# A decoder's second self-attention: last norm by pairs, output weights rounded earlier, and some diagonals made by VectorE

## The chip, the cores and the metric

One core of a Trainium2 chip runs the whole kernel in one launch. TensorE (PE) multiplies; VectorE (DVE), ScalarE (ACT) and GpSimd (POOL) compute elementwise; SyncE (SP) issues most of the DMAs, ACT and POOL some. Each engine runs its own instructions in order and waits on semaphores. The metric is the device time of one execution in microseconds, less is better; the time of the kernel before is the median of three runs.

## The reference

Two post-norm decoder layers on x of 8 sequences x 128 tokens x 256 features, with a context of the same shape. Each layer is self-attention, cross-attention and a feed-forward part, each followed by `x = layernorm(x + part)`. Layer 0 has its own kinds of these. The part that matters here is layer 1:

```python
def _L1_attn_ref(x, w_qkv, w_o):            # 16 heads of 128, no mask
    q, k, v = split(x @ w_qkv)
    scores = einsum('bhqd,bhkd->bhqk', q, k) / sqrt(128)
    probs = softmax(scores)
    values = einsum('bhqk,bhkd->bhkd', probs, v)   # v times the column sums of probs
    return values @ w_o
def _L1_xattn_ref(q, k, v):                 # 8 heads of 16 rows, q = x, k = v = context
    sm = softmax(einsum('bdm,bdn->bmn', qh, kh) * scale)
    return einsum('bmn,bcn->bcm', sm, vh)
def _L1_ffn_ref(x, gate_w, w13, w2):        # 64 experts, the best 8 of each token
    ...
```

In the attention `values` sums probs over the queries only, so a head gives `v` times a column sum.

## The kernel before, in words

Each engine's program is a chain of stages: layer 0, attention 1, cross 1, experts, combine. There is no scheduler: the order on each engine is the order of the code, and semaphores (`t.name(n)`: wait until n events) tie the engines together.

**Attention 1** (`pe_attention1`, `act_attention1`, `dve_attention1`, `pool_attention1`, `sp_attention1`, L758 to L966) loops over 16 heads, for all 8 sequences at once in two halves of 4. Products that need full precision are made of three fp32r products, of a rounded part `_hi` and a rest `_lo`. In a head TensorE makes the scores (L814), adds the head before to the output (`add_head`, L794), projects q and k of the next head, makes the column sums (L824), and projects v of the next head. ScalarE copies `sums`, rounds `oT` to `o_hi` (L874) and, last, `wo` to `wo_hi` (L876). VectorE multiplies `oT` and makes `o_lo` (L929). GpSimd makes `w_lo` of the next head and `wo_lo`. The output of all heads stands in the PSUM banks 0 to 3, a pair of sequences in each. After the last head VectorE adds each bank to `x_all` (L935) and takes statistics (L938); then come eight aggregates (L941), the variance of all (L943), one root on GpSimd (L966), and eight normalizations (L946), which give the events `x4`.

**Cross 1** (L1072 to L1381) goes by quarters: a sequence has four, 32 in all. The engines run over slots `s` of the same number: scores of quarter s, maxima (`topc`, L1252) of s, exponentials (`softc`, L1210) of s, the reciprocal of the row sums (`rsumc`, L1257) of s-1, a diagonal matrix of them (`diagc`, L1372, on GpSimd) of s-1, the turn of s-2 (softc times diagc, which transposes and scales), and its copies (`pTc`, L1264 and L1218). At fixed slots later come values, residual and norm, the gate's logits (L1313), the choice of experts (`choose`, L1271), the place of each token (`place`, L1284, which ends with `index_all`, L1294), and the scatters of the rows into the slots of the experts: 8 indirect DMAs a sequence, issued by GpSimd, two a slot (L1363). GpSimd's program per slot is: diagonal, root of a norm (slots 7+4b), scatters (slots 13+4b to 16+4b). TensorE's bank for `topc` is one of 0 to 3.

GpSimd's set-up of cross 1 (`pool_cross1_setup`: clears `kpair` and `vpair`, makes constants) stands behind attention 1, SP's loads of the context (8 DMAs for `kpair` and one for `ctx` a sequence) wait for it, and `pe_cross1` begins when all eight `x4` are there. The experts wait until all scatters have landed.

Of the kernel before, what the change touches and what calls it, by code (L numbers as in the profile page):

```python
# [719 lines left out]
class Attention1:  # L720
    def __init__(self, m):
# [31 lines left out]
        self.var_set, self.x4 = ev.compute("dve", "var_set", 1), ev.compute("dve", "x4", NSEQ)  # L753
        self.w_lo_set, self.wo_lo_set = ev.compute("pool", "w_lo_set", 3 * H1), ev.compute("pool", "wo_lo_set", H1)
        self.root = ev.compute("pool", "root4", 1)


def sp_attention1(m, a, t, te):  # L758
# [73 lines left out]
def act_attention1(m, t):  # L832
# [24 lines left out]
    for h in range(H1):  # L857
# [18 lines left out]
        act.copy(t.wo_hi[:, :], t.wo[:, :]).then_inc(*t.wo_hi_set.one)  # L876
# [4 lines left out]
def dve_attention1(m, t):  # L881
# [17 lines left out]
    for h in range(H1):  # L899
# [30 lines left out]
        if h < H1 - 1:  # L930
            half0(h + 1, 2, t.vT)
    for k in range(4):
        x = m.x_all[:, 2 * k:2 * k + 2, :].rearrange("p b d -> p (b d)")
# [8 lines left out]
    dve.wait_ge(*c)  # L942
    dve.tensor_scalar(t.var[:, :], t.mv[:, :, 1], EPS, None, ALU.add).then_inc(*t.var_set.one)  # L943
    dve.wait_ge(*t.root(1))
    for b in range(NSEQ):
        dve.tensor_scalar(m.x_all[:, b, :], m.x_all[:, b, :], t.mv[:, b, 0:1], t.rstd[:, b:b + 1],  # L946
                          ALU.subtract, ALU.mult).then_inc(*t.x4.one)


def pool_attention1(m, t):  # L950
# [13 lines left out]
def pool_attention1_root(m, t):  # L964
    m.pool.wait_ge(*t.var_set(1))
    m.pool.tensor_tensor(t.rstd[:, :], t.var[:, :], m.power[:, 0:NSEQ], ALU.pow).then_inc(*t.root.one)  # L966
# [40 lines left out]
class Cross1:  # L1007
# [18 lines left out]
    def signals(self, m):  # L1026
        ev = m.ev
        self.gate_in = ev.dma("gate_in", 1)
# [13 lines left out]
        self.setup, self.diag_set, self.root5 = ev.compute("pool", "setup", 1), pool("cdiag", 4), pool("root5", 1)  # L1042
# [28 lines left out]

def sp_cross1(m, a, t, r, te, t1):  # L1072
    sp = m.sp
    sp.wait_ge(*t.setup(1))
    for b in range(NSEQ):
        n, L = b % LANES, t.lanes[b % LANES]
        if b >= LANES:
            sp.wait_ge(*t.cs_ps(8 * (b - 1)))
        for h in range(HX):
            rows = slice(h * HDX, (h + 1) * HDX)  # L1080
            sp.dma_start(L.kpair[rows, h % 2, :], a["ctx_in"][b, rows, :]).then_inc(*t.kpair_in[n].one)
        if b >= LANES:
            sp.wait_ge(*t.ctxT_ps(b - 1))
        sp.dma_start(L.ctx[:, :], a["ctx_in"][b, :, :]).then_inc(*t.ctx_in[n].one)
        if b == 0:
            sp.dma_start(r.gate[:, :, :], a["gatew"]).then_inc(*t.gate_in.one)
        if b == 1:
            after_attention1(sp, t1)
        if b >= 1:
            sp_kept_weights(m, a, te, b)  # L1090


def pe_cross1(m, t, r, t1):
    pe, mm, tr = m.pe, m.mm, m.tr
    pe.wait_ge(*t.setup(1))
    pe.wait_ge(*t1.x4(NSEQ))

    def scores(s):
        b, mo, g0 = quarter(s)
        L = t.lanes[b % LANES]  # L1100
        pe.wait_ge(*t.xq(b + 1))
# [141 lines left out]
def dve_cross1(m, t, r):  # L1243
# [111 lines left out]
def pool_cross1(m, t, r, t0):  # L1355
# [10 lines left out]
    for s in range(CROSS_SLOTS + 3):  # L1366
        if 0 <= s - 1 < QUARTERS:
            q = s - 1
            pool.wait_ge(*t.inv(q + 1))
            if q >= 2:  # L1370
                pool.wait_ge(*t.cT_ps(2 * (q - 2) + 2))
            pool.tensor_tensor(t.diag[q % 2][:, :, :], spread(m.ident[:, :], 4, 1), spread(t.rsum[q % 3][:, :], P, 2),  # L1372
                               ALU.mult).then_inc(*t.diag_set.one)
# [476 lines left out]
class Stages:  # L1850


    def __init__(self, m, ctx):
# [14 lines left out]
        self.tc.signals(m)  # L1868
# [63 lines left out]
```

## Time and profile before

| | us |
|---|---|
| median of 3 runs | 1078.04 |
| lowest, highest | 1076.23, 1080.29 |
| the profiled execution | 1069.34 |
| its span, first to last instruction | 1067.8 |
| TensorE busy | 842.4 (79%) |
| VectorE busy | 618.8 (58%) |
| GpSimd busy | 354.0 (33%) |
| ScalarE busy | 344.5 (32%) |
| attention 1, by the timeline | about 344 to 602 |
| cross 1, to the landing of its last scatter | about 602 to 773 |
| experts and combine | about 773 to 1068 |

A stage's share of the engines says little by itself: the engines take turns, and what counts is which wait ends last at each place. Times in the rows are microseconds from the start of the span.

### The profile page before, as it was taken

How to read it: one execution, taken by the hardware profiler on the slowest of the kernel's cores; microseconds unless marked ns; L12 is line 12 of the kernel's file. 1: busy time of each engine (PE TensorE's matmuls, PEld its weight loads, DVE VectorE, ACT ScalarE, POOL GpSimd, SP SyncE). 2: the span in 40 equal slices, each digit the busy share in tenths (PEclk: the TensorE clock that was granted, in tenths of full speed). 3: DMA queues.
4: the chain of work that ended last, by engine and by line, in shares of the span. 5: the costliest groups of instructions: out<-in, count | busy, mean ns of one | idle time of the engine just before them, and what ended most of it. 6: DMA issues, size and time to landing. Idle time of an engine off the chain costs nothing.

```text
span 1067.8 us, 16943 instructions
## 1 busy us (share of the span) xinstructions
PE 842.4 (79%) x5555; PEld 689.6 (65%) x5555; DVE 618.8 (58%) x1857; ACT 344.5 (32%) x946; POOL 354.0 (33%) x396
## 2 busy tenths in 40 slices
PE   5377888879786999999998599896099988899700
PEld 2256766557455888888887376664088877788600
DVE  4184564673853566666667567785155555544477
ACT  0032222232222343444434266663033333333200
POOL 1121312312211211222111325776645555555501
PEclk9998998998988999999999699998589999999955
DMA  9900000000000112221110233461248788854254
GB/s 238 334 11 10 1 11 11 1 20 1 1 1 34 58 43 69 70 70 52 53 41 11 67 110 100 149 236 69 109 116 281 241 260 247 285 145 135 83 209 143
DMA packets 62533, 110.12 MB, mean 103 GB/s; under 512 B 11227, under 2 KB 41417, under 8 KB 61040
## 3 DMA queue, kind: packets, MB, share of 16 engines
q1 hardware_dynamic: 32064, 64.22, 19.1%
q10 hardware_dynamic: 21216, 27.48, 8.6%
q0 software_dynamic: 9168, 17.35, 4.4%
q8 instruction: 45, 0.74, 0.3%
q14 instruction: 40, 0.33, 0.1%
HBM read 94.50 MB, written 35.52 MB: 122 GB/s over the span
## 4 chain that ended last, share of the span: by engine, by line
PE 60%; issue 13%; DVE 11%; POOL 6%; ACT 3%; DMA 2%; ACTq 1%; SPq 1%; another core or an unknown queue 1%; DVEq 0%; POOLq 0%
PE ps L152 57%; PE ps L155 4%; DVE acco L1778 3%; POOL kheads L677 2%; POOL x_slots L1363 2%; ACTq L447 1%; DVE soft L551 1%; DMA bdn_sb<-in_bdn 1%; DVE top L549 1%; SPq L286 1%; POOL mv L169 1%; DVE topc L1252 0%; DMA rowso<-y_slots 0%; POOL mvo L169 0%
## 5 line engine op out<-in xcount | busy, mean ns | idle before, releaser
L1723 POOL DMA_INDIRECT y_slots<-o_e,index_e x127 | 124.4, 979 | 116.6 <-DVE o_e L1712 80.2
L152 PE MATMUL ps<-xT_e,w_slot 128*128 128x128 f32 x760 | 101.7, 277 | 3.6 <-ACT xT_e L1662 2.1
L1704 DVE TENSOR_TENSOR h_e<-ps,gate_e 128x128 f32<-128x128 f32 x127 | 37.0, 291 | 108.2 <-ACT gate_e L1668 66.7
L152 PEld LDWEIGHTS ps<-xT_e,w_slot 128*128 128x128 f32 x760 | 92.4, 192 | 5.7 <-ACT xT_e L1662 3.2
L152 PEld LDWEIGHTS ps<-diagc,softc 128*128 128x128 f32 x512 | 62.2, 199 | 33.0 <-POOL diagc L1372 25.0
L152 PE MATMUL ps<-diagc,softc 128*128 128x128 f32 x512 | 68.2, 289 | 8.7 <-DVE pTc L1264 4.9
L1662 ACT COPY xT_e<-ps 128x256 f32<-128x256 f32 x127 | 47.2, 372 | 82.1 <-PE ps L155 63.1
L959 POOL TENSOR_TENSOR wo_lo<-wo,wo_hi 128x256 fp32r<-128x256 f32 x15 | 14.0, 932 | 176.0 <-ACT wo_hi L876 176.0
L1210 ACT ACTIVATE softc<-ps,topc 128x256 f32<-128x256 f32 x128 | 59.0, 476 | 40.4 <-DVE topc L1252 36.6
L152 PE MATMUL ps<-w_slot,h_e 128*128 128x256 f32 x190 | 59.5, 395 | 14.4 <-DVE h_e L1704 8.6
L1363 POOL DMA_INDIRECT x_slots<-rows_all,index_all x64 | 63.8, 997 | 18.0 <-issue 15.9
L155 PE MATMUL ps<-ident,rows_e 128*128 128x128 f32 x254 | 49.5, 277 | 21.9 <-DMA rows_e<-x_slots 21.9
L677 POOL TENSOR_TENSOR kheads<-k,headmask 128x1024 f32<-128x1024 f32 x16 | 38.1, 2404 | 86.3 <-ACT k L457 86.3
L1668 ACT ACTIVATE gate_e<-ps 128x128 f32<-128x128 f32 x127 | 35.5, 279 | 96.0 <-PE ps L152 88.7
L152 PE MATMUL ps<-x_hi,w_hi 128*128 128x512 f32 x192 | 61.8, 404 | 5.2 <-POOL w_lo L955 5.2
L169 POOL TENSOR_TENSOR mv<-mv,power 128x1 f32<-128x1 f32 x24 | 13.2, 548 | 157.6 <-DVE mv L165 157.6
L152 PE MATMUL ps<-x_lo,w_hi 128*128 128x512 f32 x192 | 59.8, 393 | 0.0
L152 PE MATMUL ps<-x_hi,w_lo 128*128 128x512 f32 x192 | 59.7, 392 | 0.0
L155 PEld LDWEIGHTS ps<-ident,rows_e 128*128 128x128 f32 x254 | 35.8, 143 | 34.4 <-DMA rows_e<-x_slots 22.1
L1712 DVE COPY o_e<-ps 128x256 f32<-128x256 f32 x127 | 52.9, 417 | 3.4 <-issue 1.5
L1252 DVE TENSOR_REDUCE topc<-ps 128x2 f32<-128x512 f32 x64 | 41.0, 684 | 17.9 <-PE ps L152 17.7
L1372 POOL TENSOR_TENSOR diagc<-ident,rsumc 128x512 f32<-128x512 f32 x32 | 33.3, 1041 | 45.2 <-DVE rsumc L1257 44.2
(263 smaller groups left out, 2015.1 us busy)
## 6 DMA issues: line engine op xcount, KB each, us to landing
w_slot<-in_we SPq DMA_DIRECT2D x71, 384.0 KB
rows_e<-x_slots SPq DMA_DIRECT2D x69, 136.0 KB
w_slot<-in_we ACTq DMA_DIRECT2D x24, 384.0 KB
x_slots<-blank ACTq DMA_DIRECT2D x4, 2176.0 KB, 15.8
rowso<-y_slots SPq DMA_DIRECT2D x8, 1024.0 KB, 5.0
rows_e<-x_slots ACTq DMA_DIRECT2D x58, 136.0 KB
w_kept<-in_we SPq DMA_DIRECT2D x20, 384.0 KB
wh<-in_wqkv SPq DMA_DIRECT2D x16, 384.0 KB, 3.4
```

The costliest lines, as they stand in the source:

```text
L152: return self.pe.matmul(out, lhsT, rhs, start=start, stop=stop, skip_group_check=shared)
L155: return self.pe.transpose(out, in_, self.ident[:, :])
L677: pool.tensor_tensor(L.kheads[:, mo, :, :], spread(L.k[:, mo, :], HP, 1), spread(m.headmask[:, :], P, 2), ALU.mult).then_inc(*t.kheads.one)
L1210: last = act.activation(soft[:, j, e, :], bank[:, e * D:(e + 1) * D], ACT.Exp, bias=top[:, c], accum_out=rsum[:, c])
L1252: dve.tensor_reduce(t.top[s % 3][:, 2 * j:2 * j + 2], t.s_bank[2 * (s % 2) + j].rearrange("p (e n) -> p e n", e=2), AX.X, ALU.max, negate= ...
L1363: pool.indirect_dma_start(m.x5_slots, bass.IndirectOffsetOnAxis(ap=r.index[:, b, j:j + 1], axis=0), r.rows[:, b, :], None).then_inc(*t.row ...
L1372: pool.tensor_tensor(t.diag[q % 2][:, :, :], spread(m.ident[:, :], 4, 1), spread(t.rsum[q % 3][:, :], P, 2), ALU.mult).then_inc(*t.diag_se ...
L1662: act.copy(T.xT[:, :, :].rearrange("p k t -> p (k t)"), T.t_bank[:, 0:D]).then_inc(*t.rowsT.one)
L1668: act.activation(T.gate[:, :], T.g_bank[:, 0:P], ACT.Silu).then_inc(*t.gate.one)
L1704: dve.tensor_tensor(T.h[:, :], T.g_bank[:, P:2 * P], T.gate[:, :], ALU.mult).then_inc(*t.h.one)
L1712: dve.tensor_copy(T.o[:, :], T.o_bank[:, 0:D]).then_inc(*t.o.one)
L1723: pool.indirect_dma_start(m.y_slots, bass.IndirectOffsetOnAxis(ap=T.index[:, :], axis=0), T.o[:, :], None, bounds_check=TOK * TOPK - 1, oo ...
```

## The change

In attention 1:
- VectorE takes each pair of sequences through addition, statistics, aggregates and variance at once; GpSimd takes the root of each pair; VectorE normalizes pair k-1 behind the variance of pair k. `var_set` and `root` have four events instead of one.
- TensorE's last `add_head` waits for the first half of `o_lo` only, where it needs no more.
- ScalarE rounds `wo` to `wo_hi` ahead of the two copies of the sums instead of behind `o_hi`; the wait for `y_ps` moves there with it.
- GpSimd's set-up of cross 1 moves into head 4, and SP's loads of the gate and of the first two contexts (19 DMAs) into head 8.

In cross 1:
- TensorE no longer waits for all `x4`: scores of quarters 0 and 1 wait for the variances of the pairs whose banks they overwrite, and through ScalarE's scaled copy for their sequence.
- GpSimd makes diagonals 0 to 12 and VectorE 13 to 31, each behind its reciprocal.

```diff
 def add_head(h, sequences):
-        pe.wait_ge(*t.o_lo_set(2 * h + 2))
+        pe.wait_ge(*t.o_lo_set(2 * h + 1 + sequences[-1] // 4))
...
 act_attention1
+        if h:
+            act.wait_ge(*t.y_ps(h))
+        act.wait_ge(*t.wo_in(h + 1))
+        act.copy(t.wo_hi[:, :], t.wo[:, :]).then_inc(*t.wo_hi_set.one)
         for half in range(2):
             cols = slice(512 * half, 512 * half + 512)
             act.wait_ge(*t.sums_ps(2 * h + half + 1))
             act.copy(t.sums[:, cols], t.sbank[half]).then_inc(*t.sums_set.one)
             act.wait_ge(*t.oT_set(2 * h + half + 1))
-            if h:
-                act.wait_ge(*t.y_ps(h))
             act.copy(t.o_hi[:, cols], t.oT[:, cols]).then_inc(*t.o_hi_set.one)
-        act.wait_ge(*t.wo_in(h + 1))
-        act.copy(t.wo_hi[:, :], t.wo[:, :]).then_inc(*t.wo_hi_set.one)
...
 dve_attention1
+    def norm_end(k):
+        dve.wait_ge(*t.root(k + 1))
+        for b in (2 * k, 2 * k + 1):
+            dve.tensor_scalar(m.x_all[:, b, :], m.x_all[:, b, :], t.mv[:, b, 0:1], t.rstd[:, b:b + 1],
+                              ALU.subtract, ALU.mult).then_inc(*t.x4.one)
     for k in range(4):
...
         c = chain(dve.tensor_tensor(x, x, m.ps[:, k, :], ALU.add))
         dve.wait_ge(*c)
         for b in (2 * k, 2 * k + 1):
             c = chain(dve.bn_stats(t.stats[:, b, :], m.x_all[:, b, :]))
-    dve.wait_ge(*c)
-    for b in range(NSEQ):
-        c = chain(dve.bn_aggr(t.mv[:, b, :], t.stats[:, b, :]))
...
+        dve.wait_ge(*c)
+        for b in (2 * k, 2 * k + 1):
+            c = chain(dve.bn_aggr(t.mv[:, b, :], t.stats[:, b, :]))
+        dve.wait_ge(*c)
+        dve.tensor_scalar(t.var[:, pair], t.mv[:, pair, 1], EPS, None, ALU.add).then_inc(*t.var_set.one)
+        if k:
+            norm_end(k - 1)
+    norm_end(3)
...
 pool_attention1
     for h in range(H1):
+        if h == H1 // 4:
+            cross1_setup()
...
 pool_attention1_root
+    for k in range(NSEQ // 2):
+        pair = slice(2 * k, 2 * k + 2)
+        m.pool.wait_ge(*t.var_set(k + 1))
+        m.pool.tensor_tensor(t.rstd[:, pair], t.var[:, pair], m.power[:, pair], ALU.pow).then_inc(*t.root.one)
...
+SCATTERS_FROM = 13
...
 sp_attention1, in the loop over heads
+        if h == H1 // 2:
+            sp_cross1_first(m, a, tc, r)
...
 pe_cross1
     pe.wait_ge(*t.setup(1))
-    pe.wait_ge(*t1.x4(NSEQ))
+    pe.wait_ge(*t1.half1(3 * H1))
+    pe.wait_ge(*t1.sums_set(2 * H1))
     def scores(s):
...
+        if s < 2:
+            pe.wait_ge(*t1.var_set(2 * s + 2))
...
 dve_cross1
     def inverse(s):
         dve.wait_ge(*t.exp(s + 1))
         dve.reciprocal(t.rsum[s % 3][:, :], t.rsum[s % 3][:, :]).then_inc(*t.inv.one)
+        if s >= SCATTERS_FROM:
+            dve.wait_ge(*t.inv(s + 1))
+            dve.wait_ge(*t.cT_ps(2 * (s - 2) + 2))
+            dve.tensor_tensor(t.diag[s % 2][:, :, :], spread(m.ident[:, :], 4, 1), spread(t.rsum[s % 3][:, :], P, 2),
+                              ALU.mult).then_inc(*t.diag_dve.one)
...
 pool_cross1
-        if 0 <= s - 1 < QUARTERS:
+        if 0 <= s - 1 < SCATTERS_FROM:
```

## Rows read from the trace of the kernel before

**Rows 1.** The page, part 4: shares of the chain that ended last, by engine.

```profile
PE 60%; issue 13%; DVE 11%; POOL 6%; ACT 3%; DMA 2%; ACTq 1%; SPq 1%; another core or an unknown queue 1%; DVEq 0%; POOLq 0%
```

**Rows 2.** Busy time by stretch, its columns in the first line.

```profile
core 0: us, PE busy (x) PEld busy (x) DVE busy (x) ACT busy (x) POOL busy (x), PEclk, DMA share, GB/s
600.00:610.00 10.00, 5.00 (x15) 1.65 (x16) 5.42 (x14) 4.03 (x17) 1.04 (x1) 0.50 0.42 138
700.00:720.00 20.00, 18.27 (x174) 13.17 (x175) 15.97 (x44) 13.72 (x54) 15.10 (x17) 1.00 0.72 278
```

**Rows 3.** The chain in order of time (start, us, what), end of attention 1.

```profile
589.50 1.64 PE ps L152 x6
...
597.73 1.66 POOL rstd L966
...
599.41 2.69 DVE x_all L946 x8
...
604.91 0.68 DVE topc L1252
```

**Rows 4.** Timeline of VectorE there: start, us, engine, line, instruction [idle <-releaser].

```profile
588.08 0.69 DVE L929 TENSOR_TENSOR o_lo<-oT,o_hi 128x512 fp32r<-128x512 f32 x1 [0.68 <-ACT o_hi L874]
...
591.16 0.69 DVE L935 TENSOR_TENSOR x_all<-x_all,ps 128x512 f32<-128x512 f32 x1 [2.38 <-PE ps L152]
...
596.01 0.75 DVE L938 BATCH_NORM_STATS2 stats<-x_all 128x6 f32<-128x256 f32 x2
...
596.80 0.64 DVE L941 BATCH_NORM_AGGREGATE mv<-stats 128x2 f32<-128x6 f32 x8
...
597.47 0.17 DVE L943 TENSOR_SCALAR var<-mv 128x8 f32<-128x8 f32 x1
```

**Rows 5.** The chain in order of time: turns of slots 14 and 30 in cross 1.

```profile
655.25 6.66 PE ps L152 x72
...
722.88 4.73 PE ps L152 x56
```

**Rows 6.** Timeline of cross 1, slots 19 to 22.

```profile
678.08 0.17 DVE L1257 RECIPROCAL rsumc<-rsumc 128x4 f32<-128x4 f32 x1
678.16 0.66 DVE L1264 COPY pTc<-ps 128x512 f32<-128x512 f32 x1
...
684.34 1.29 DVE L1252 TENSOR_REDUCE topc<-ps 128x2 f32<-128x512 f32 x2 [0.33 <-PE ps L152]
...
686.48 1.65 DVE L1294 TENSOR_SCALAR index_all<-rows_all 128x8 uint32<-128x8 f32 x1
...
687.04 1.06 POOL L1372 TENSOR_TENSOR diagc<-ident,rsumc 128x512 f32<-128x512 f32 x1
...
689.07 2.02 PE L152 MATMUL ps<-diagc,softc 128*128 128x128 f32 x16 [1.13 <-DVE pTc L1264]
```

**Rows 7.** Timelines of ScalarE, VectorE and GpSimd in head 13 of attention 1.

```profile
558.64 0.58 ACT L870 COPY sums<-ps 128x512 f32<-128x512 f32 x1 [0.31 <-PE ps L152]
...
562.49 0.40 ACT L876 CAST wo_hi<-wo 128x256 fp32r<-128x256 f32 x1
...
562.62 0.69 DVE L929 TENSOR_TENSOR o_lo<-oT,o_hi 128x512 fp32r<-128x512 f32 x1 [0.69 <-ACT o_hi L874]
...
562.96 0.93 POOL L959 TENSOR_TENSOR wo_lo<-wo,wo_hi 128x256 fp32r<-128x256 f32 x1 [11.88 <-ACT wo_hi L876]
```

**Rows 8.** Groups of VectorE by shape: busy us, mean ns | idle before, releaser.

```profile
L927 DVE TENSOR_TENSOR oT<-vT,sums 128x512 f32<-128x512 f32 x32 | 22.0, 688 | 26.9 <-ACT sums L870 26.9
...
L560 DVE TENSOR_TENSOR soft<-soft,rsum 128x1024 f32<-128x1024 f32 x16 | 20.4, 1277 | 0.6
```

**Rows 9.** Timeline of VectorE, the place of sequence 0, GpSimd idle meanwhile.

```profile
654.14 0.17 DVE L1294 TENSOR_SCALAR index_all<-rows_all 128x8 uint32<-128x8 f32 x1
```

**Rows 10.** Timeline, then chain, at the end of cross 1.

```profile
743.81 0.23 DVE L1313 TENSOR_REDUCE onec<-ps 128x1 f32<-128x64 f32 x1 [6.35 <-remote]
...
745.18 0.57 POOL L169 TENSOR_TENSOR mvc<-mvc,power 128x1 f32<-128x1 f32 x1 [2.71 <-DVE mvc L165]
...
770.17 2.45 DMA x_slots<-rows_all,index_all
```

More of the change, by code:

```diff
@@ L752, in __init__, with sp_attention1 @@
         self.oT_set, self.o_lo_set = dve("oT_set", 2), dve("o_lo_set", 2)
-        self.var_set, self.x4 = ev.compute("dve", "var_set", 1), ev.compute("dve", "x4", NSEQ)
+        self.var_set, self.x4 = ev.compute("dve", "var_set", NSEQ // 2), ev.compute("dve", "x4", NSEQ)
         self.w_lo_set, self.wo_lo_set = ev.compute("pool", "w_lo_set", 3 * H1), ev.compute("pool", "wo_lo_set", H1)
-        self.root = ev.compute("pool", "root4", 1)
-def sp_attention1(m, a, t, te):
+        self.root = ev.compute("pool", "root4", NSEQ // 2)
+        self.cross1_setup = ev.compute("pool", "cross1_setup", 1)
+def sp_attention1(m, a, t, te, tc, r):
     sp = m.sp
@@ L931, in dve_attention1 @@
             half0(h + 1, 2, t.vT)
+    def norm_end(k):
[3 more added lines that the diff above has]
+                              ALU.subtract, ALU.mult).then_inc(*t.x4.one)
     for k in range(4):
-        x = m.x_all[:, 2 * k:2 * k + 2, :].rearrange("p b d -> p (b d)")
+        pair = slice(2 * k, 2 * k + 2)
+        x = m.x_all[:, pair, :].rearrange("p b d -> p (b d)")
         dve.wait_ge(*t.out_ps(k + 1))
@@ L938, in dve_attention1, with pool_attention1 @@
             c = chain(dve.bn_stats(t.stats[:, b, :], m.x_all[:, b, :]))
-    dve.wait_ge(*c)
-    for b in range(NSEQ):
-        c = chain(dve.bn_aggr(t.mv[:, b, :], t.stats[:, b, :]))
[L942 to L950, printed above, removed]
+        dve.wait_ge(*c)
[6 more added lines that the diff above has]
+    norm_end(3)
+def pool_attention1(m, t, cross1_setup):
     pool = m.pool
     for h in range(H1):
+        if h == H1 // 4:
+            cross1_setup()
         for which in range(3):
@@ L964, in pool_attention1_root @@
 def pool_attention1_root(m, t):
-    m.pool.wait_ge(*t.var_set(1))
-    m.pool.tensor_tensor(t.rstd[:, :], t.var[:, :], m.power[:, 0:NSEQ], ALU.pow).then_inc(*t.root.one)
+    for k in range(NSEQ // 2):
+        pair = slice(2 * k, 2 * k + 2)
+        m.pool.wait_ge(*t.var_set(k + 1))
+        m.pool.tensor_tensor(t.rstd[:, pair], t.var[:, pair], m.power[:, pair], ALU.pow).then_inc(*t.root.one)
 def after_attention1(engine, t):
@@ L1024, in __init__, with signals @@
         self.logits = self.rank = m.ps[:, 7, 0:NE]
-    def signals(self, m):
+    def signals(self, m, setup):
         ev = m.ev
+        self.setup = setup
         self.gate_in = ev.dma("gate_in", 1)
@@ L1069, in of_slot, with sp_context, sp_cross1_first @@
     return b if rest == 0 and 0 <= b < NSEQ else None
+def sp_context(m, a, t, b):
+    sp = m.sp
+    n, L = b % LANES, t.lanes[b % LANES]
+    if b >= LANES:
+        sp.wait_ge(*t.cs_ps(8 * (b - 1)))
+    for h in range(HX):
+        rows = slice(h * HDX, (h + 1) * HDX)
+        sp.dma_start(L.kpair[rows, h % 2, :], a["ctx_in"][b, rows, :]).then_inc(*t.kpair_in[n].one)
+    if b >= LANES:
+        sp.wait_ge(*t.ctxT_ps(b - 1))
+    sp.dma_start(L.ctx[:, :], a["ctx_in"][b, :, :]).then_inc(*t.ctx_in[n].one)
+def sp_cross1_first(m, a, t, r):
+    m.sp.wait_ge(*t.setup(1))
+    m.sp.dma_start(r.gate[:, :, :], a["gatew"]).then_inc(*t.gate_in.one)
+    for b in range(LANES):
+        sp_context(m, a, t, b)
 def sp_cross1(m, a, t, r, te, t1):
[L1073 to L1076, printed above, removed]
+    after_attention1(m.sp, t1)
+    for b in range(1, NSEQ):
         if b >= LANES:
[L1078 to L1090, printed above, removed]
+            sp_context(m, a, t, b)
+        sp_kept_weights(m, a, te, b)
 def pe_cross1(m, t, r, t1):
@@ L1109, in turn @@
     def turn(s):
-        pe.wait_ge(*t.diag_set(s + 1))
+        if s < SCATTERS_FROM:
+            pe.wait_ge(*t.diag_pool(s + 1))
+        else:
+            pe.wait_ge(*t.diag_dve(s - SCATTERS_FROM + 1))
         for j in range(2):
@@ L1372, in pool_cross1 @@
             pool.tensor_tensor(t.diag[q % 2][:, :, :], spread(m.ident[:, :], 4, 1), spread(t.rsum[q % 3][:, :], P, 2),
-                               ALU.mult).then_inc(*t.diag_set.one)
+                               ALU.mult).then_inc(*t.diag_pool.one)
         b = of_slot(s, 7)
```

10 lines of the change are left out of this document (5 added, 5 removed).

## Prediction

> **What bounds the kernel now.** First the page's chain of work that ended last [rows 1]: TensorE carries 60% of it, so VectorE, ScalarE and GpSimd matter only where TensorE waits for them. Then the busy time in stretches [rows 2]. From 600 to 610 us TensorE is busy 5.00 of 10 us, at a granted clock of 0.50, the level of 1.2 GHz. From 700 to 720, in the cross attention, it is busy 18.27 of 20 at full clock, with VectorE at 15.97 and GpSimd at 15.10: three engines near full, coupled by waits. The chain in order of time [rows 3] and the timeline [rows 4] show the hand-over between the two stages. The last head's additions start at 589.50, when `wo_lo` is ready; VectorE adds and takes statistics of four pairs; then comes one root for all (597.73, 1.66 us), eight normalizations (599.41, 2.69 us), scores, and the first `topc` at 604.91. Last come the periods of the cross attention: four sequences pass from the turn at 655.25 to that at 722.88, 16.91 us each [rows 5], and the timeline of one of them, up to 689.07 [rows 6].
>
> **Part 1, the norm by pairs.** VectorE's last `o_lo` starts at 588.08 and takes 0.69 [rows 4]; independent work can start 0.62 behind it, so pair 0 begins at 588.70 instead of 591.16: the new order has `wo_lo` ready long before and lets TensorE add sequences 0 to 3 as soon as the first half of `o_lo` is there, about 586.8. TensorE's first six matmuls took 1.64 us [rows 3], so pair 0 is there in time, and each later pair before VectorE comes to it. One pair costs VectorE 0.72 for the addition (0.69 and a gap) and 0.79 for two statistics (596.01 to 596.80), then for the new small steps: two aggregates, 0.19 (eight took 0.64, so 0.08 each, and a drain of about 0.03), and the variance, 0.08 until the next can start (0.17 in full) [rows 4]. That is 1.78. Two normalizations add 2/8 of 2.69, 0.67, less overlap: 0.65 [rows 3]. GpSimd's root of two columns lies between 0.57 for one column [rows 10] and 1.66 for eight [rows 3]; on that line 0.57 + (1.66 - 0.57)/7 = 0.73. It hides behind the next pair (1.70 us) except for the last. So: start 588.70; pair 0 1.78; pairs 1 to 3 with the norm of the one before, 3 x 2.43 = 7.29; root 4 exposed, 0.09 + 0.08 + 0.73 + 0.03 = 0.93 less 0.65 hidden under norm 2, 0.28; norm 3, 0.65. Sum 598.70. The copy of `vpair` (0.40) follows, then the first `topc` at 599.1. Its scores wait for variance 2 (592.35, so banks 0 and 1 are read), for x4(1) (592.7) and its scaling by ScalarE, and are done before 596, even at half clock. Before, `topc` began at 604.91: a shift of **-5.8 us**.
>
> What may take from it is the clock. Before, TensorE worked at 1.2 GHz in all of 600 to 610 [rows 2]. TensorE will idle as long between its first scores and the rest, so it starts low again; if it stays low 1 us longer, 0.5 us is lost. I take 0.5 off, bounds -0.3 to +1.3: **-5.3 us**.
>
> The cover: the 19 DMAs for context and gate, and GpSimd's set-up, cost nothing where they now stand. SP issues the DMAs in head 8, behind that head's weights, under 0.5 us each, so 9 us, and SP's next wait comes a head (14.9 us) later; `wo` and `wh` of head 9 are queued behind and start after that wait anyway. GpSimd's set-up (3.5 us) stands at head 4 behind `wo_lo` and ahead of `w_lo`; GpSimd was idle 11.88 us in a head [rows 7]. If that cover were gone, head 4 would lose at most 3.5 us, once.
>
> **Part 2, `wo_hi` ahead of the sums.** In a late head [rows 7] ScalarE idles 0.31 before `sums`; a 0.40 copy placed there delays `sums` by about 0.1. Behind it stand both `sums`, both `o_hi` and half 1 of `vT`; VectorE's `oT` waits for them. But the 0.40 is gone at 562.49, so `vT` isn't later. GpSimd's `wo_lo` (0.93) moves from 562.96 to about 558.7 and now meets VectorE's `oT`, which follows `sums` at 559.2. `o_lo` ends at 563.31; `wo_lo`, which the same matmuls need, ended at 563.89 and TensorE did not wait for it. So at least 0.58 us of slack covers the 0.1 and a collision. Cost 0, bounds 0 to 0.2 us a head, 3 us over 15 heads. The new wait for `y_ps` is met before `qT` is copied; it holds nothing.
>
> **Part 3, VectorE makes diagonals 13 to 31.** GpSimd's takes 1.06 us [rows 6]. On VectorE the nearest rows are `oT` (two SBUF operands, 128x512), 0.688, and `soft*rsum` (the same broadcast, 128x1024), 1.277, half of which is 0.64 [rows 8]. I take 0.69, of which 0.61 pass until the next instruction can start (so with `o_lo` behind which `vT` is copied, 562.62 to 563.22). The reciprocal of 678.08 (0.17) let the next instruction start 0.08 behind it [rows 6]; now the diagonal needs its result, 0.17 and a gap of 0.04. So 0.21 + 0.61 - 0.08 = 0.74 each. The path of a sequence runs from one turn over the scores, `topc`, `pTc`, the residual and norm, the choice and the placing back to the next `pTc`. Three of the four diagonals lie on it (slots 3, 0 and 1); the fourth, in slot 2, lies beside TensorE's turn, values and gate. So +2.22. Of this 0.38 vanishes in VectorE's wait before `topc` at 684.34 [rows 6] (0.33 in the row, and 0.05 as the copy before it can overlap). Gained is the hold of `index_all`: 1.65 at 686.48, until GpSimd's diagonal of 687.04 ended at 688.10, against 0.17 with GpSimd idle [rows 6, 9], so 1.48. 16.91 + 2.22 - 0.38 - 1.48 = 17.27, +0.36 a sequence, and over the four periods +1.4. GpSimd then has 8 scatters of 1.27 us in 17 us; it isn't late. In the last two quarters VectorE is 0.7 later behind one diagonal, and TensorE no longer waits for GpSimd's, which stood behind two scatters: +0.1. **Part 3: +1.5 us.** Bounds: if VectorE were no bound at all, the 1.13 us for which TensorE waited for `pTc` at 689.07 [rows 6] would go, 15.78 a sequence, -4.5 in all; with a diagonal at GpSimd's own 1.06 it is (1.06 - 0.69) x 12 more, +5.9.
>
> **What doesn't move.** From the root of sequence 7 (745.18) GpSimd has twenty scatters, 25 us, up to 770.17 [rows 10]. Four are of sequence 5, behind that root by program order, and sixteen of 6 and 7. That root waited for VectorE, not for GpSimd, so freeing GpSimd earlier brings nothing here. The experts start behind the last landing, so the whole shift of sequence 7 reaches the end.
>
> **The sum.** -5.3 + 0 + 1.5 = -3.8. The profiled execution took 1069.34 us (its span 1067.8), the three timed ones 1078.04 in the median, 8.7 more: the working stands on the faster one, and I carry the difference over: 1078.04 - 3.8 = 1074.2 us.
>
> **The rivals.**
> (a) The 6.4 us that VectorE waited for the gate's logits near the end [rows 10] have no maker in the trace. TensorE's gate matmuls were recorded as ended at 740.98, 2.8 us before VectorE began at 743.81. If they are an accident that new timing doesn't repeat: -6.6, 1071.4 us. For: no other sequence shows it. Against: nothing in the edit touches it. Chance 0.17.
> (b) The period falls half-way to TensorE's own 15.78, to 16.3, since VectorE had 4 us of idle time in 20: -5.3 - 2.3 = -7.6, 1070.4. For: stretch 700 to 720 [rows 2]. Against: the idle time stood in slot 2, the new work in slots 3, 0 and 1. Chance 0.12.
> (c) Attention pays: `wo_lo` beside `oT` eats the slack of `o_lo`, 0.2 us in each of 15 heads, or the start keeps half of its gain: +3, 1077.2. This is also the case that the change hardly does what it says. Chance 0.20.
> (d) The other side: VectorE's diagonals are held by GpSimd's scatters, as `index_all` was held. It has two SBUF operands and comes while a scatter of 0.96 us may run. If each of the 12 on the path is held for a whole scatter, +0.96 x 12 = 11.5: 1085.7. It decides from 0.32 us a diagonal (no gain left), and makes it over 0.5% slower from 0.77. Against: `oT` keeps 0.688 over 32 uses [rows 8]. Chance 0.07. The Trainium skill speaks for this rival: "GPSIMD Engine Reference", Key points, says that GpSimd and VectorE share their SBUF interfaces and contend where a VectorE instruction has two SBUF inputs. By that rule in full the time would be this rival's; the trace agrees for GpSimd's arithmetic (the hold up to 688.10) and shows no such hold by a scatter.
> The forecast keeps 0.44, its own range 1071.5 to 1077.
>
> **How the numbers follow.** 0.5%, about what a measurement of this kernel can tell from no change, is 5.4 us: faster means under 1072.7. That is (a) and (b) for the most part, 0.24, and 0.11 of the forecast's lower edge: 0.35. Slower, over 1083.4: (d) and a sliver, 0.07. Within: 0.58. The range takes in (a), (b) and (c) with the bounds of part 3, and leaves out (d): 1067.5 to 1080.0.
>
> **What the profile after would show.** Part 1: VectorE's first `topc` 5 to 6 us sooner, statistics and norms interleaved, `rstd` four times at about 0.73. Part 2: heads still 14.9 us apart, TensorE without idle time before `wo_hi`. Part 3: 17.3 us from turn to turn, `index_all` at 0.17, VectorE's diagonals at 0.69 and TensorE's wait for `pTc` longer, not shorter. I am wrong if a diagonal takes over 0.9, if heads take over 15.0, or if the 25 us of scatters after the last root shrink.

## The result, and the profile after

Six runs of each on the same chip: 1083.76 us in the median (1082.03 to 1087.12) against 1076.20 (1075.26 to 1080.29), a ratio of 1.0056 with a 95% interval of 1.0036 to 1.0076. The change made the kernel 7.6 us slower. The forecast, 1074.2 us with a range up to 1080.0, was wrong, and in sign.

The two profiled executions (1069.34 and 1082.03 us, spans 1067.8 and 1080.5), taken apart at the same instructions:

| stretch | before | after | difference |
|---|---|---|---|
| start to the first `sums` copy of attention 1 | 364.93 | 362.44 | -2.5 |
| to the `sums` copy of head 15 | 219.18 | 215.66 | -3.5 |
| to the first `topc` | 20.78 | 15.30 | -5.5 |
| to the root of sequence 7 | 140.29 | 159.12 | +18.8 |
| to TensorE's first expert matmul | 29.56 | 29.75 | +0.2 |
| to its last `rows_e` transpose | 230.74 | 235.87 | +5.1 |
| to the end | 62.28 | 62.33 | 0 |

The first and the sixth lines belong to code that the change doesn't touch: the first came out between 360.4 and 364.9 in all traces, the sixth between 227.1 and 240.2 in twelve traces from chips of this kind. The loss is the fourth line.

The start is as forecast. Timeline of VectorE after the change, pair 3 and the first `topc` (start, us, engine, line, instruction [idle <-releaser]), then one root on GpSimd:

```profile
589.56 0.68 DVE L946 TENSOR_TENSOR x_all<-x_all,ps 128x512 f32<-128x512 f32 x1
590.27 0.75 DVE L949 BATCH_NORM_STATS2 stats<-x_all 128x6 f32<-128x256 f32 x2
591.06 0.25 DVE L952 BATCH_NORM_AGGREGATE mv<-stats 128x2 f32<-128x6 f32 x2
591.35 0.17 DVE L954 TENSOR_SCALAR var<-mv 128x2 f32<-128x2 f32 x1
591.42 0.73 DVE L939 TENSOR_SCALAR x_all<-x_all,mv,rstd 128x256 f32<-128x256 f32 x2
592.41 0.73 DVE L939 TENSOR_SCALAR x_all<-x_all,mv,rstd 128x256 f32<-128x256 f32 x2 [0.26 <-POOL rstd L980]
593.07 0.42 DVE L1339 COPY vpairc<-ps 128x256 f32<-128x256 f32 x1
593.40 2.47 DVE L1283 TENSOR_REDUCE topc<-ps 128x2 f32<-128x512 f32 x4
```

```profile
591.60 0.78 POOL L980 TENSOR_TENSOR rstd<-var,power 128x2 f32<-128x2 f32 x1 [1.73 <-DVE var L954]
```

The diagonals are as forecast too. Timeline of VectorE in slots 16 and 17 of cross 1, where [rows 6] has one sequence of the kernel before:

```profile
677.43 1.28 DVE L1283 TENSOR_REDUCE topc<-ps 128x2 f32<-128x512 f32 x2
678.63 0.17 DVE L1288 RECIPROCAL rsumc<-rsumc 128x4 f32<-128x4 f32 x1
678.83 0.71 DVE L1292 TENSOR_TENSOR diagc<-ident,rsumc 128x512 f32<-128x512 f32 x1
679.46 0.68 DVE L1300 COPY pTc<-ps 128x512 f32<-128x512 f32 x1
682.00 1.29 DVE L1283 TENSOR_REDUCE topc<-ps 128x2 f32<-128x512 f32 x2 [1.86 <-remote]
683.20 0.17 DVE L1288 RECIPROCAL rsumc<-rsumc 128x4 f32<-128x4 f32 x1
683.40 0.69 DVE L1292 TENSOR_TENSOR diagc<-ident,rsumc 128x512 f32<-128x512 f32 x1
```

A diagonal takes 0.69 to 0.71 us, the next instruction starts 0.61 behind. The new thing is the wait of 1.86 us at 682.00, by a releaser that the profile calls remote, as at the end of the kernel before [rows 10]. `topc` needs the scores. TensorE's timeline there:

```profile
676.61 1.08 PE L152 MATMUL ps<-pTc,vpairc 128*32 128x128 f32 x32
...
677.78 1.13 PE L152 MATMUL ps<-kpairc,xqc 32*128 32x512 f32 x4
680.28 2.02 PE L152 MATMUL ps<-diagc,softc 128*128 128x128 f32 x16 [1.38 <-issue]
684.48 0.41 PE L155 MATMUL ps<-ident,rows_all 128*128 128x128 f32 x2 [2.17 <-DVE slotc L1324]
...
686.00 3.61 PE L152 MATMUL ps<-diagc,softc 128*128 128x128 f32 x16
```

The scores stand recorded from 677.78 for 1.13 us, but `topc` got them at 682.00. The semaphore events of the trace show why: the values (676.61, ended 677.69) gave their signal at 681.89, 4.20 us late, and what was behind them, scores too, followed at 0.04 to 0.05 us each. Before it was 0.58 to 0.65 us at this place, and 0.04 where no scatter was running. The profile models the ends of matmuls, so this lateness can be in the signal or in the work itself; what is measured is that whoever waits for it starts late. GpSimd's timeline beside it:

```profile
676.08 1.16 POOL L1399 DMA_INDIRECT x_slots<-rows_all,index_all  x1 [0.20 <-issue]
677.55 0.96 POOL L1399 DMA_INDIRECT x_slots<-rows_all,index_all  x1 [0.30 <-issue]
678.81 0.96 POOL L1399 DMA_INDIRECT x_slots<-rows_all,index_all  x1 [0.30 <-issue]
680.08 0.96 POOL L1399 DMA_INDIRECT x_slots<-rows_all,index_all  x1 [0.30 <-issue]
```

The signal came 0.85 us behind the end (681.04) of four scatters in a row. With its diagonals gone, GpSimd runs four scatters where it ran two. It repeats in each sequence (654.97 to 659.49, 698.51 to 702.76, 719.32 to 723.52). A second cost comes with the first: TensorE waits 2.17 us for `slotc` (0.22 in the trace of after_again, below), the granted clock is 0.50 from 686.17 to 689.58, and the turn at 686.00 takes 3.61 us instead of 2.02. Busy time by stretch after the change (columns as in [rows 2], the clock is the number before the last two):

```profile
660.00:680.00 20.00, 17.61 (x142) 12.09 (x141) 14.09 (x39) 10.20 (x39) 7.51 (x8) 0.77 0.27 78
680.00:700.00 20.00, 17.23 (x154) 12.76 (x154) 13.57 (x39) 9.57 (x37) 7.93 (x9) 0.91 0.38 126
700.00:720.00 20.00, 16.67 (x154) 12.79 (x154) 14.21 (x38) 10.25 (x39) 8.07 (x9) 0.91 0.66 246
```

So 1.86 of wait and 1.59 of a slower turn are 3.45 of the 3.53 us by which a period of 20.82 is over the 17.29 of the same code without lateness (below). Periods were 22.8, 22.7, 21.1 and then 20.8 us. That the clock falls because of this wait is an argument from the order of the two: in three traces it also fell once without a late signal (below the table).

### The profile page after: what moved, and what is told of

The parts are those of the page before. It is cut to its first block, busy times and chain, and to the rows that moved or that the text cites. A ratio compares the mean times of both kernels' runs of the same rounds, so it can differ in the third digit from the quotient of the medians.

```text
span 1080.5 us, 16927 instructions
## 1 busy us (share of the span) xinstructions
PE 846.6 (78%) x5547; PEld 692.2 (64%) x5555; DVE 626.6 (58%) x1879; ACT 345.2 (32%) x946; POOL 332.4 (31%) x380
## 4 chain that ended last, share of the span: by engine, by line
PE 59%; DVE 13%; issue 12%; POOL 6%; ACT 3%; DMA 2%; ACTq 2%; SPq 1%; another core or an unknown queue 1%; POOLq 0%; DVEq 0%
PE ps L152 54%; PE ps L155 4%; DVE acco L1814 3%; POOL kheads L677 2%; POOL x_slots L1399 2%; ACTq L447 1%; DVE soft L551 1%; DMA bdn_sb<-in_bdn 1%; DVE top L549 1%; SPq L286 1%; DVE topc L1283 1%; POOL mv L169 1%; DVE pTc L1300 1%; ACT gate_e L1704 1%
## 5 line engine op out<-in xcount | busy, mean ns | idle before, releaser
L152 PEld LDWEIGHTS ps<-diagc,softc 128*128 128x128 f32 x512 | 67.5, 213 | 34.4 <-issue 21.5
L152 PE MATMUL ps<-diagc,softc 128*128 128x128 f32 x512 | 73.6, 303 | 9.1 <-DVE pTc L1300 4.6
L155 PEld LDWEIGHTS ps<-ident,rows_e 128*128 128x128 f32 x254 | 35.9, 143 | 35.4 <-DMA rows_e<-x_slots 22.9
L967 POOL TENSOR_TENSOR w_lo<-wh,w_hi 128x256 fp32r<-128x256 f32 x48 | 34.0, 734 | 69.3 <-ACT w_hi L846 69.3
L152 PE MATMUL ps<-kpairc,xqc 32*128 32x512 f32 x128 | 40.2, 707 | 7.3 <-DVE var L954 4.8
```

Of the source, the lines that this page charges most:

```text
L152: return self.pe.matmul(out, lhsT, rhs, start=start, stop=stop, skip_group_check=shared)
L155: return self.pe.transpose(out, in_, self.ident[:, :])
L967: pool.tensor_tensor(t.w_lo[h % 2][:, :, which, :], t.wh[h % 2][:, :, which, :], t.w_hi[h % 2][:, :, which, :], ALU.subtract).then_inc(*t. ...
```

## The experiments

The expectations weigh two theories. The hold: a run of scatters on GpSimd holds back TensorE's signal. The load: VectorE's added diagonals themselves take the time.

The runs of one group were made on one chip and share runs of the kernel before. In three groups the kernel before took 1032 to 1033 us, and in the profiles of these groups every signal of the values came 0.04 us behind its matmuls (0.07 at most): I call such chips prompt. In the other three, and in the comparison above, it took 1068 to 1077 us and signals came late beside scatters: late chips. That sorts everything that follows. The words name what was seen at the time: the record gives the same chip, number 4, for a prompt group (pool_diags) and for a late one about 20 minutes later (held_after), so this may be a state and not a property of the chip. The kernel before was profiled on a late chip alone. Lateness is from the end of the values to their semaphore event, in slots 16, 20, 24 and 28; a period is from one sequence's values to the next's.

| kernel | chip | GpSimd between scatters | lateness, us | period, us | ratio (95%) |
|---|---|---|---|---|---|
| before | late | diagonals | 0.6 | 16.91 | 1 |
| after | late | 0.30 us | 4.2 to 4.5 | 20.8 to 22.8 | 1.0056 (1.0036 to 1.0076) |
| after_again | prompt | 0.30 us | 0.04 | 17.29 (one place +1.4) | 0.9935 (0.9919 to 0.9951) |
| pool_diags | prompt | diagonals | 0.04 | 16.91 | 0.9922 (0.9904 to 0.9939) |
| pool_diags_2 | prompt | diagonals | 0.04 | 16.91 | 0.9918 (0.9901 to 0.9935) |
| pool_diags_3 | late | diagonals | 0.6 to 0.8 | 16.91 | 0.9869 (0.9848 to 0.9891) |
| dve_diags_only | prompt | 0.30 us | 0.04 | 17.29 | 1.0022 (1.0009 to 1.0035) |
| dve_diags_only_2 | prompt | 0.30 us | 0.04 | 17.29 | 1.0008 (0.9995 to 1.0021) |
| scatters_behind | prompt | no scatters | 0.04 | 17.24 (one place +3.0) | (longer end) |
| scatters_behind_2 | late | no scatters | 0.04 | 17.24 (one place +3.0) | (longer end) |
| short_spacer | late | 0.30 us, memset in it | 2.6 to 4.5 | 19.5 to 22.6 | 1.0038 (1.0017 to 1.006) |
| spaced_2 | prompt | product | 0.04 | 20.3 to 20.6 | 1.0046 (1.0029 to 1.0062) |
| spaced_3 | late | product | 1.3 to 1.4 | 20.4 to 20.7 | 1.0021 (1.0002 to 1.004) |
| paced | late | 0.56 us or more | 1.3 to 1.7 | 17.3 to 20.6 | 0.9964 (0.9943 to 0.9985) |
| held_pool_diags | late | diagonals, product | 0.6 | 16.48 | 0.9884 (0.9843 to 0.9924) |
| held_after, _2, _3 | late | 0.30 us | 3.4 to 4.6 | 20.7 to 22.9 | 1.0067, 1.0069, 1.0077 |
| wo_hi_ahead | late | diagonals | 0.6 | 16.91 | (one run) |

The +1.4 and +3.0 stand at the same place, between the values of slots 24 and 26. No signal of the values was late there; TensorE waited 1.7 us for `pTc` instead of 1.4, and the granted clock was 0.50 from 694.21 to 697.63 (after_again) and from 694.50 to 701.33 (scatters_behind_2).

**Parts 1 and 2 alone** (pool_diags).

```diff
-SCATTERS_FROM = 13
+SCATTERS_FROM = 32
```

> The kernel after with all 32 diagonals made by GpSimd again: parts 1 and 2 alone. Both theories of the 20.8 to 22.4 us periods (the hold: a run of scatters back to back on GpSimd holds back TensorE's signal behind the values until about 0.9 us after the run; the load: VectorE's diagonals themselves take that time) expect the period of 16.9 us again, topc 5.5 us sooner than in the kernel before, and so about 5.5 us less than before, a ratio of 0.995. If instead the earlier start is given back later whatever makes the diagonals, the ratio is 1.000.

Again on another prompt chip (pool_diags_2, with after_again) and on a late one (pool_diags_3, with spaced_3):

> The kernel after with all diagonals made by GpSimd again, as in pool_diags. On a chip with late signals the hold expects the run of pairs as in the kernel before, signals at most 0.7 us late, periods of 16.9 us, 5.5 us less than before: 0.995. On a chip without them 0.992 again.

> Parts 1 and 2 alone. On a chip with late signals: as in before, late by 0.4 to 0.7 us, 16.9 us a period, 5 to 8 us less than before, 0.992 to 0.995. On a chip without: 0.992 for the third time. The kernel held_pool_diags stood at 0.988 on a chip with late signals, with periods of 16.5 us; the difference to this one is then what its spare product gave by moving GpSimd's diagonal off index_all.

7.5 and 8.9 us less on prompt chips, 13.1 on a late one. So everything but VectorE's diagonals pays, and more than the 5.5 that I expected. GpSimd on the late chip (profile of pool_diags_3), where the values end at 673.39:

```profile
671.03 1.19 POOL L1398 DMA_INDIRECT x_slots<-rows_all,index_all  x1 [0.19 <-issue]
672.52 0.96 POOL L1398 DMA_INDIRECT x_slots<-rows_all,index_all  x1 [0.30 <-issue]
673.83 1.04 POOL L1407 TENSOR_TENSOR diagc<-ident,rsumc 128x512 f32<-128x512 f32 x1 [0.34 <-issue]
675.02 1.01 POOL L1398 DMA_INDIRECT x_slots<-rows_all,index_all  x1 [0.16 <-issue]
```

Their signal came at 674.03, 0.64 late. This is the version that beats both: on either kind of chip it is under the kernel before, and on the late one, beside held_after_2 of the same group (1084.43 us), it took 1064.10.

**Part 3 alone** (dve_diags_only): the kernel before with `SCATTERS_FROM = 13` and the edits of `inverse`, `turn` and `pool_cross1` from the change.

> The kernel before with VectorE's diagonals 13 to 31 alone: part 3 without parts 1 and 2. The forecast had this part at +1.5 us (ratio 1.001). Both the hold and the load expect what the kernel after lost: periods of 20.8 to 22.4 us, about +13 us, a ratio of 1.012. If the loss came from the earlier start together with the diagonals, it is less than +5.

And again, as the last run (dve_diags_only_2):

> The kernel before with VectorE's diagonals 13 to 31 alone, once more, on whatever chip this call gets. On a chip with late signals the step that failed in the forecast should show by itself: signals 4 us late, periods of 20.8 to 22.8 us, 17 to 19 us more than before, a ratio of 1.015 to 1.019. On a chip without: 17.29 us a period and 1.002 again. If it stays under 1.010 on a chip with late signals, the loss needs the earlier start or the moved set-up too.

Not +13 us but +2.4 and +0.2 in two groups: the first miss, since both chips were prompt. One fact settles what the forecast did well. From the profile of dve_diags_only, the values of two sequences on TensorE, and `index_all`:

```profile
662.88 1.08 PE L152 MATMUL ps<-pTc,vpairc 128*32 128x128 f32 x32
...
680.17 1.08 PE L152 MATMUL ps<-pTc,vpairc 128*32 128x128 f32 x32
```

```profile
669.22 0.17 DVE L1304 TENSOR_SCALAR index_all<-rows_all 128x8 uint32<-128x8 f32 x1
```

17.29 us a period, where the forecast had 17.27. Part 3 never ran alone on a late chip. What it costs there is taken from kernels that also have parts 1 and 2: 159.12 us from the first `topc` to the last root in after, 139.72 in pool_diags_3. That it would cost as much without them is not shown.

**The kernel after again** (after_again), unchanged.

> The kernel after, unchanged. On the chip of the first three experiments no signal came late in any trace, and their terms were those of the forecast (norm by pairs 8 us less, VectorE's diagonals 17.29 us a period). The hold as a property of the chip: where the trace shows the signal behind the values 0.04 us after their end, the ratio to before is 0.9922 x 1.0022 = 0.994, periods 17.3 us, and the kernel before needs about 1032 us; where it shows it late by 4 us, the ratio is 1.006, periods 20.8 to 22.4 us, and the kernel before needs about 1076 us. The hold as a property of this kernel alone (parts 1 and 3 together make it): 1.006 and late signals on either chip.

0.9935, 6.2 us less: the very change of the title is a gain here. In the same group pool_diags_2 took 1023.90 us and after_again 1026.65, so part 3 still cost 2.7. Four scatters run in a row beside the values as before, and no signal is late. From its profile, GpSimd's run, TensorE's values, and VectorE's `topc` behind:

```profile
671.33 1.16 POOL L1399 DMA_INDIRECT x_slots<-rows_all,index_all  x1 [0.20 <-issue]
672.80 0.96 POOL L1399 DMA_INDIRECT x_slots<-rows_all,index_all  x1 [0.30 <-issue]
674.06 0.96 POOL L1399 DMA_INDIRECT x_slots<-rows_all,index_all  x1 [0.30 <-issue]
675.33 0.96 POOL L1399 DMA_INDIRECT x_slots<-rows_all,index_all  x1 [0.30 <-issue]
```

```profile
671.86 1.08 PE L152 MATMUL ps<-pTc,vpairc 128*32 128x128 f32 x32
```

```profile
675.31 1.27 DVE L1283 TENSOR_REDUCE topc<-ps 128x2 f32<-128x512 f32 x2
```

The scatters take the same 0.96 us with the same gaps of 0.30 as on the late chip. What differs is only TensorE's signal.

**No scatters beside cross 1** (scatters_behind on a prompt chip, scatters_behind_2 on a late one): all 64 are issued behind the root of sequence 7.

```diff
-        for late in range(4):
-            b = of_slot(s, 13 + late)
-            if b is not None:
-                scatter(b, 2 * late, 2)
+    for b in range(NSEQ):
+        scatter(b, 0, TOPK)
```

> The kernel after with all 64 scatters issued behind the root of sequence 7 instead of 20, so that GpSimd has no scatter during the attention. The time rises by about 44 x 1.27 = 56 us at the end and says nothing; the period does. The hold: VectorE's waits for late signals before topc vanish, the period is 17.3 us as forecast. The load: it stays at 20.8 us, and topc still waits.

> The kernel after with all scatters behind the root of sequence 7, on whatever chip this call gets. If scatters on GpSimd are what makes the signals late, then also on a chip where the kernel before needs 1065 us or more no signal of the values is late before the last root and the period is 17.2 to 17.3 us. If such a chip is late for another reason (the expert weights that SP loads meanwhile, a slower TensorE), signals are late by 2 to 4 us there with no scatter running, and the period is over 19 us.

On the prompt chip the period was 17.24 us (20.28 at the place named below the table), and no signal of the values late. On the late chip it was the same, with VectorE making the diagonals: the scatters make the lateness, not the chip's TensorE and not the loads of the weights, and VectorE's load does not make the 20.8 us. One execution was taken on each chip.

**What ends it** (short_spacer, spaced, paced): GpSimd does something, or nothing for a while, between pairs of scatters.

```diff
 short_spacer, behind each pair
+                m.pool_chain(pool.memset(t.spare[:, 0, 0:1], 0.0))
 spaced, where a diagonal was made
+            pool.wait_ge(*t.inv(s))
...
+            m.pool_chain(pool.tensor_tensor(t.spare[:, :, :], spread(m.ident[:, :], 4, 1), spread(m.ident[:, 0:4], P, 2), ALU.mult))
 paced, at the same place
+            pool.wait_ge(*t.inv(s))
```

> The kernel after with one memset of a single column (0.13 us as the row of line_no shows) on GpSimd behind each pair of scatters up to slot 34. On a chip with late signals: if any instruction that is not a scatter ends the hold, signals are at most 0.7 us late, periods 17.3 us, ratio 0.995; if it takes a time without scatters of about 0.9 us, it stays at 20.8 us and 1.006. On a chip without late signals it costs at most 4 x 0.2 us a period and stands within 0.002 of the 0.9935 of the kernel after.

> The kernel after, VectorE still making diagonals 13 to 31, but GpSimd computes a 128x512 product into a spare tile at each place where it made a diagonal before. Nothing waits for it. On a chip with late signals the hold expects the runs of scatters to be broken into pairs again, signals at most 0.7 us late, periods of 17.3 to 18.8 us (18.8 if index_all is held by GpSimd's product again, 1.5 us), a ratio of 0.992 to 1.002; the load expects 20.8 us and 1.006 or more. On a chip without late signals the product can only cost: the period between 17.3 and 18.8 us, ratio 0.994 to 1.000.

> The kernel after with GpSimd's 128x512 product into a spare tile at each place of a moved diagonal. On the chip without late signals it was 1.0046 against before. On a chip with late signals: the runs are pairs again; if a break of 1 us is enough, where 0.13 us was not, signals are at most 1.1 us late and the ratio lies at or under 1.006, since the product's hold on VectorE costs here what it cost there; if only the end of the scatters counts, whatever stands between them, signals are 4 us late, and the ratio is 1.015.

> The kernel after, but GpSimd waits in each slot from 14 to 32 for the reciprocal of that slot (the event it waited for before, when it made the diagonal) and computes nothing there: pairs of scatters at the old pace, with idle time between them. On a chip with late signals: if a run ends by time without a scatter, signals are 0.4 to 1.4 us late instead of 4, the period is 17.3 to 17.9 us, and the ratio 0.990 to 0.995; if the gaps are too short to end it, signals stay over 2 us late and the ratio over 1.000. On a chip without late signals nothing changes against after: 0.9935.

The memset fits into the gap that scatters leave anyway (profile of short_spacer, GpSimd):

```profile
677.03 0.96 POOL L1400 DMA_INDIRECT x_slots<-rows_all,index_all  x1 [0.30 <-issue]
677.99 0.12 POOL L1422 MEMSET spare<- 128x1 f32 x1
678.29 0.96 POOL L1400 DMA_INDIRECT x_slots<-rows_all,index_all  x1 [0.19 <-issue]
```

From 677.99 to 678.29 are the same 0.30 us, and signals are as late. In paced the gap is 0.56 us:

```profile
673.33 0.96 POOL L1399 DMA_INDIRECT x_slots<-rows_all,index_all  x1 [0.30 <-issue]
674.85 1.28 POOL L1399 DMA_INDIRECT x_slots<-rows_all,index_all  x1 [0.56 <-issue]
```

and the signal of values that ended at 673.06 came at 674.72, 0.43 behind the second scatter, in the gap. So an idle GpSimd ends the hold too: at this place a gap of 0.30 us did not let the signal through and one of 0.56 did. It is no threshold. Near the end of the stage signals came in the middle of a run with gaps of 0.30: in the profile of after, that of the values which ended at 739.73 came at 742.77, 0.31 into the fourth scatter of a run. Paced is 0.9 points better than after on chips of this kind (0.9964 against 1.0056), but misses its own expectation of 0.990 to 0.995: from the first `topc` to the last root it takes 149.33 us, half-way between pool_diags_3 and after, and signals of its second values (slots 14, 18 and 30) still come up to 2.6 us late.

Spaced shows what the product costs. Its lateness fell to 1.3 us on the late chip, and its period was 20.3 us or more on either kind of chip, over the 18.8 that I had as the most. VectorE and GpSimd, profile of spaced_2:

```profile
681.01 1.73 DVE L1327 TENSOR_TENSOR slot_all<-slotc,chosenc 128x64 f32<-128x64 f32 x1
681.59 1.05 POOL L1415 TENSOR_TENSOR spare<-ident 128x512 f32<-128x512 f32 x1
```

1.73 us instead of 0.23, up to 0.10 behind the product's end, as `index_all` was held [rows 6]. The Trainium skill, "GPSIMD Engine Reference", Key points, has GpSimd and VectorE contend where the VectorE instruction has two SBUF inputs, and `slot_all` has two; the ends of the two rows agree with it. Their starts don't explain it: by the records `slot_all` began 0.58 us ahead of the product and should have been done. The rest of the period's excess was not taken apart; the granted clock was 0.50 from 684.16 to 687.57 in it.

**The lateness made by hand** (held_after, held_pool_diags): a 0.8 us product on GpSimd behind the run of scatters, and VectorE's `topc` of slots 17, 21, 25 and 29 waits for it. The edit of held_after (held_pool_diags has `late == 2` in its place, and `SCATTERS_FROM = 32`):

```diff
+                if late == 3 and b < 4:
+                    pool.tensor_tensor(t.spare[:, 0:3, :], ...).then_inc(*t.freed.one)
...
+        b = of_slot(s, 17)
+        if b is not None and b < 4:
+            dve.wait_ge(*t.freed(b + 1))
```

> The kernel after, with the late signal made by hand. Behind the fourth scatter in a row of sequences 0 to 3 GpSimd computes a 128x384 product into a spare tile (about 0.8 us, so that it ends where the late signals of the trace of after came, 0.85 us behind the run), and VectorE's topc of slots 17, 21, 25 and 29 waits for it, as it waited for the late signal. If the late signal is enough to explain the loss, then on a chip without late signals the periods are 20.8 to 22.4 us instead of 17.3, TensorE's clock falls to 0.5 once in each, and the kernel takes about 4 x 3.9 = 15 us more than the kernel after there: a ratio to before of 1.006 to 1.010. If something else made the loss, the wait is met sooner or is absorbed, and the ratio stays under 1.000.

> The kernel after with VectorE's topc of slots 17, 21, 25 and 29 waiting for a 0.8 us product behind GpSimd's fourth scatter. The first run of it met a chip with late signals, where its wait ended with the late signal itself and changed nothing (1.0067, beside 1.0056 of after). On a chip without late signals it tests whether the lateness alone is enough: periods of 20.8 to 22.4 us, ratio to before 1.006 to 1.010 where after has 0.9935. If not enough, under 1.000.

> As held_after and held_after_2, which both met chips with late signals. On a chip without: if the lateness alone is enough, periods of 20.8 to 22.4 us and a ratio to before of 1.006 to 1.010, where after had 0.9935; if not, under 1.000. On a chip with late signals again 1.007.

> The same rule in the kernel with all diagonals on GpSimd: the same product and the same wait, behind the pair of scatters of slots 15, 19, 23 and 27, which is as far as the run goes there, since a diagonal follows. If the diagonals between the scatters are what protected the kernel before, VectorE waits little or nothing here: GpSimd has 0.8 us more work in a period, periods are 16.9 to 17.7 us, ratio 0.992 to 0.996. If the place of the wait costs as such, whatever the run's length, it loses what the experiment before it loses, 1.004 or more.

held_after met late chips all three times. Its wait ended just after the late signal would have, periods were those of after, and so it is inconclusive: that lateness alone makes the whole loss is argued from the sum of 3.45 us above and was not shown on a prompt chip. held_pool_diags, where diagonals part the scatters, lost nothing; it was faster than its own expectation of 0.992 to 0.996, with periods of 16.48 us. The spare product moves GpSimd's next diagonal off `index_all`, which took 0.18 us there instead of 1.65. The stage did not gain by that: 141.19 us from the first `topc` to the last root, against 139.72 in pool_diags_3.

**Part 2 alone** (wo_hi_ahead), a single execution.

> The kernel before with wo_hi ahead of the copies of the sums alone: part 2 by itself. From the sums of head 0 to those of head 15 the kernel before takes 219.2 us and the kernel after 215.7, in every trace of either. If TensorE's 0.19 us of idle time ahead of each head's first wo_hi product was a wait for wo_lo, which this edit brings forward, this kernel shows 215.7 to 216.5; if the gain came from the other edits of attention 1, 219.2.

215.66 us from head 0 to head 15, as in the kernel after: it is this edit. The row in the kernel before, TensorE's weight loads:

```profile
549.11 0.19 PEld L152 LDWEIGHTS ps<-wo_hi,o_hi 128*128 128x128 f32 x1 [0.19 <-issue]
```

GpSimd's `wo_lo` ran there from 548.06 for 0.93 us, up to 548.99, and these 0.19 us of idle time are a wait for it, though the profile says issue. They are gone in wo_hi_ahead. Its first `topc` was 237.2 us behind head 0's `sums`, against 240.0 before and 231.0 after, so part 2 is worth 2.8 us in all and part 1 another 6.2.

## Why the prediction was wrong, step by step

- **Part 1, -5.3 us: right.** The stretch shrank by 5.5; roots took 0.70 to 0.79 (0.73 forecast). Taken behind part 2 alone it is 6.2. The cover held too: the heads take 215.66 us with the moved set-up and DMAs (after) and without them (wo_hi_ahead).
- **Part 2, 0 us: mis-sized.** The working said that TensorE did not wait for `wo_lo`. It did, some 0.2 us in each of 15 heads, 3.5 us by the heads and 2.8 to the first `topc`. The heads were 14.61 us apart, not 14.9 as I wrote, and became 14.38. The check that I named, no idle time before `wo_hi`, would have shown the step wrong in the kernel before already.
- **Part 3, +1.5 us: the step that failed.** Its diagonal (0.69 to 0.72), `index_all` (0.17) and period (17.29 against 17.27) were measured as forecast on chips where signals are prompt, and there the part cost 0.2, 2.4 and 2.7 us. On the chip of the comparison the stretch from the first `topc` to the last root grew by 18.8 us. The failed sentence is "GpSimd then has 8 scatters of 1.27 us in 17 us; it isn't late." It puts at nothing what these scatters do to the others, without a row that shows it: I priced the diagonals that GpSimd loses only as load taken off it. They also parted its scatters. With them the signals of the values in slots 16, 20, 24 and 28 came within 0.65 us, without them after 4.2 to 4.5. No bound of mine (-4.5 to +5.9) had a case in which an emptier GpSimd harms TensorE. None of my three signs of being wrong came true either (diagonals 0.71, heads 14.38, the scatters after the last root unchanged): the period, 20.8 us where I had 17.3, would have been the one to name.
- **Rival (a), 0.17: the clue, misread.** The 6.35 us by a remote releaser [rows 10] had a maker: the signal of the values that ended at 740.39 came at 743.72, beside six scatters in a row from 735.14 to 742.47. "No other sequence shows it" was true because no other had such a run. On prompt chips 2.75 and 3.56 us remain of that wait (pool_diags, pool_diags_2), but GpSimd's queue of scatters then holds the root: it follows 140.25 and 137.55 us behind the first `topc`, against 140.29 before.
- **Rival (d), 0.07: wrong mechanism, nearly the right time (1085.7).** No VectorE diagonal was held by a scatter; the longest took 0.71 in the profile of after and 0.76 in any. What scatters hold is TensorE's signal.
- **What doesn't move: right**, 29.56 us from the last root to the experts before, 29.75 after.

The sum with measured terms: -3.5 - 5.5 + 18.8 = +9.8, to set against +7.6 in the medians and, with the two untouched stretches, +12.7 between the profiles.

## What to carry to other kernels

Before taking work off an idle-looking engine, ask what its instructions part: here moving the diagonals from between GpSimd's indirect DMAs to VectorE cost 19 us on late chips and under 3 on prompt ones, and putting other work or a pause in their place gave only a part back. A wait whose releaser the profile calls remote, behind an engine that had long been done, is a mechanism with no name yet, not an accident: find what ran on all queues meanwhile, and ask where the change makes more of it. And a kernel with many scatters should be compared on more than one chip and at more than one time; the same edit was 0.65% faster in one comparison and 0.56% slower in another.

## What the runs showed of the hardware

- In some groups of runs a run of indirect DMAs on GpSimd (0.96 us each, 0.30 apart) holds back the completion signal of TensorE's values matmuls and all signals behind it, as a rule until 0.4 to 1.3 us after the run's end or a longer gap. Some came earlier, one 0.02 us behind the run's end (held_after_3, at 659.73) and some in the middle of a run (after, at 742.77). The matmuls' records and the scatters' own look the same as in groups without it (0.04 us). Why it is so in one group and not in another isn't known.
- Other matmuls can be held too. In the profile of before the transposes of `rows_all` that ended at 686.88 gave their signal 0.64 us late, beside the scatter of 686.03. Most turns beside scatters were not held (0.01 us), but at the end of cross 1 after the change a turn whose first half ended at 742.58 gave its signal at 745.69, 3.11 us late, and VectorE's copy of it waited:

```profile
745.72 0.69 DVE L1300 COPY pTc<-ps 128x512 f32<-128x512 f32 x1 [1.64 <-remote]
```

  What decides which matmuls are held was not tried.
- The experts' stage has 127 such scatters, and took 198 to 201 us on prompt chips and 227 to 240 on late ones, in kernels with the same code there. That it is the same hold is likely but wasn't tested. Busy time of the kernel before, then of after_again on a prompt chip (PE is the second number):

```profile
850.00:900.00 50.00, 44.85 (x331) 40.27 (x330) 28.18 (x194) 16.49 (x55) 27.00 (x28) 1.00 0.85 257
```

```profile
850.00:900.00 50.00, 48.65 (x376) 44.75 (x375) 32.48 (x220) 20.13 (x63) 31.80 (x34) 1.00 0.97 328
```
